# Building the one-hot tables of two edge sums with eight single-value comparisons per turn instead of one wide comparison

## What is computed

```
x = x + gnn0(layernorm(x))        # two layers: h = (x + mean over edges of x[col]) @ W.T + b, norm, silu
x = x + moe(layernorm(x))         # 8 experts, top 2
x = x + gnn1(layernorm(x))        # sum over edges of weight * x[src], two matrices, norm, gelu
x = x + half(layernorm(x))        # a dense part on half of the rows
```

## Time and profile before

| | us |
|---|---|
| median of three runs | 5513.28 |
| lowest and highest run | 5509.91, 5519.62 |
| the profiled execution | 5518.8 |
| its span, first to last instruction | 5517.1 |
| busy in the span: PE, DVE, POOL, ACT | 4292.8, 3152.9, 2684.9, 1286.6 |
| mean granted TensorE clock, as a share of 2.4 GHz | 0.919 |

### The profile page before, as it was taken

How to read it: one execution, slowest core, us unless ns; L and a number is a source line. 1 busy time by engine, 2 the same in 40 slices (tenths; PEclk the granted TensorE clock), 3 DMA queues, 4 the chain that set the end, 5 groups by cost and what they waited for, 6 DMA issues and landing times. The chain is left out here.

```text
span 5517.1 us, 75612 instructions
## 1 busy us (share of the span) xinstructions
PE 4292.8 (78%) x20122; PEld 3546.4 (64%) x20123; DVE 3152.9 (57%) x7387; ACT 1286.6 (23%) x3985; POOL 2684.9 (49%) x2621
## 2 busy tenths in 40 slices
PE   6588777777778888989870699999349888888459
PEld 3386655555557777878760588888237666666347
DVE  8987555555566666766672011111358777787841
ACT  0395000000054434444261122222110000001612
POOL 0003777777717777777705100000457777775121
PEclk9798999999999999999995899999669999999779
DMA  4201333333323333333312312211433333333520
GB/s 171 56 11 38 97 101 103 101 102 100 98 66 93 92 92 92 93 95 94 119 47 74 109 65 68 95 65 67 126 109 104 104 104 104 105 104 89 181 70 18
DMA packets 256142, 499.45 MB, mean 91 GB/s; under 512 B 61573, under 2 KB 149296, under 8 KB 255952
## 3 DMA queue, kind: packets, MB, share of 16 engines
q0 software_dynamic: 125632, 344.11, 21.2%
q1 hardware_dynamic: 125120, 147.87, 8.3%
q10 hardware_dynamic: 5200, 5.24, 0.3%
HBM read 490.49 MB, written 90.68 MB: 105 GB/s over the span
## 5 line engine op out<-in xcount | busy, mean ns | idle before, releaser
L1052 PE MATMUL sum_sums<-sum_got,sum_onehot 128*128 x9408 | 2233.2, 393 | 557.7 <-SPq L114 484.6
L1052 PEld LDWEIGHTS sum_sums<-sum_got,sum_onehot 128*128 128x128 f32 x9408 | 1793.6, 195 | 962.6 <-issue 719.3
L985 POOL DMA_INDIRECT sum_got<-xn,edge_row x1568 | 1539.3, 982 | 1016.8 <-DVE edge_row L1082 491.8
L1255 DVE TENSOR_TENSOR acc<-acc,sum_sums 128x256 f32 (+1 forms) x2352 | 992.0, 422 | 993.1 <-PE sum_sums L1052 739.0
L985 POOL DMA_INDIRECT sum_got<-h,edge_row x784 | 874.8, 1116 | 352.0 <-issue 238.5
L780 ACT ACTIVATE xb<-xb,edge_weight 128x98 f32<-128x98 f32 x1568 | 430.9, 362 | 633.9 <-DVE xb L750 633.3
L1795 POOL DMA_INDIRECT moe_out_c_got<-moe_out,place_i x98 | 95.8, 977 | 881.6 <-PEq L1753 852.1
L1215 DVE TENSOR_TENSOR sum_onehot<-iota,edge_local 128x1024 f32<-128x1024 f32 x396 | 482.8, 1220 | 7.3 <-PEq L2439 7.2
L2026 DVE TENSOR_TENSOR moe_f_y<-moe_f_ps_y,moe_b 128x256 f32<-128x256 f32 x112 | 42.3, 419 | 699.1 <-PE moe_f_ps_y L1961 699.1
L1210 DVE TENSOR_SCALAR sum_onehot<-iota,sum_now 128x128 f32<-128x128 f32 x1584 | 425.0, 360 | 7.5
L1961 PE MATMUL moe_f_ps_y<-xb,moe_f_hT 128*128 128x256 f32 x1792 | 428.7, 382 | 0.0
(11 more groups left out here) (482 smaller groups left out, 3702.2 us busy)
## 6 DMA issues: line engine op xcount, KB each, us to landing
xb<-in_L_ffn_W SPq DMA_DIRECT2D x112, 1024.0 KB
sum_got<-xn,edge_row POOLq DMA_INDIRECT x1568
moe_in<-acc SPq DMA_DIRECT2D x28, 512.0 KB, 6.2
moe_f_xin<-moe_in SPq DMA_DIRECT2D x56, 256.0 KB
moe_out<-moe_f_y SPq DMA_DIRECT2D x56, 256.0 KB
xn<-xb SPq DMA_DIRECT2D x14, 896.0 KB, 8.0
sum_got<-h,edge_row POOLq DMA_INDIRECT x784, 2.8
h<-xb SPq DMA_DIRECT2D x7, 896.0 KB, 4.1
```

The costliest lines, as they stand in the source:

```text
L985: pool.indirect_dma_start(got[:, c % SU, 0:D], None, source, bass.IndirectOffsetOnAxis(ap=p.edge_row[:, c:c + 1], axis=0)).then_inc(s_got[ ...
L1052: mm = nc.tensor.matmul(sums[k % 2][j], onehot[:, ((k % 2) * HALF + j) * PAIR + r, :], pair[:, r, :], start=(r == 0), stop=(r == PAIR - 1))
L1255: v.tensor_tensor(a, a, sums[k % 2][j], ALU.add).then_inc(s_added[j], 1)
```

## The change

The unweighted `build` takes the way of the weighted one. Eight values of `edge_local` are copied to `now` (one field instead of two), a wait on the copy follows, and then come eight `tensor_scalar` comparisons of 128 elements, each against one per-partition value. `now` is allocated in all three passes, with one field where there are no weights. The tables that come out are the same.

```diff
-        now = p.sb("now", [P, 2, 2, HALF * PAIR], F32, ctx) if weighted else None
+        now = p.sb("now", [P, 2, fields, HALF * PAIR], F32, ctx)
...
                 else:
-                    number = p.iota[:].unsqueeze(1).to_broadcast([P, TURN, P])
-                    local = p.edge_local[:, bass.ds(c, TURN)].unsqueeze(2).to_broadcast([P, TURN, P])
-                    ins = v.tensor_tensor(out, number, local, ALU.is_equal)
+                    v.tensor_copy(now[:, half, 0, :], p.edge_local[:, bass.ds(c, TURN)]).then_inc(s_built, 1)
+                    dve.wait_ge(s_built, built)
+                    for j in range(TURN):
+                        ins = v.tensor_scalar(out[:, j, :], p.iota[:], now[:, half, 0, j:j + 1], None, ALU.is_equal)
                 ins.then_inc(s_onehot, 1)
```

## The result

The changed kernel takes 5413.68 us (median of 4 runs, 5410.86 to 5422.98), the kernel before 5515.68 (4 runs, 5509.91 to 5519.62): a ratio of 0.9819, 95% interval 0.9802 to 0.9836, so 102 us less. The forecast was 82 us less, 5431, with a range of 5377 to 5492. The profiled execution of the changed kernel took 5422.98 us, the longest of its four; its span is 5421.2, 95.9 us shorter than before.

The account below looks back on a forecast made before the run. POOL, issuing gathers back to back, was taken to bound sum0 and sum1. 38.4 us (sum0) + 46.7 (sum1) - 2.7 (ends of the passes) = 82.4 us less, bringing the median to 5431, range 5377 to 5492.

Parts of the forecast that it names:

- What bounds the kernel: In sum0 and sum1 POOL issues gathers back to back, 1.251 us each at the median, and sets the pace.
- Rival B: sum1 keeps its length through hosted constructions or DVE and PE; only sum0 gains, 36 us, to 5478; chance 0.15.
- What the wide comparison takes: Gathers wait for comparisons of two SBUF operands, mostly L1215; whole stretch over the median 47.0 us in sum0, 133.3 in sum1.
- What the eight comparisons take: Stretch left by the new comparisons, taken from sum2: 8.6 us for each pass, bounds 0 and 34.
- one of its signs: In sum1 stretched gathers should end 0.82 us after L757 and L750, not after the new comparisons.
- set against itself: Rule that a two-port tensor_scalar fully blocks GpSimd while it runs: 25 us a pass, gain 50 us (5463).
- sum0: Pass with stretch falling from 47.0 to 8.6 us: 38.4 us less on POOL, 1.3 us lost at its start.
- sum1: Pass with 133.3 us of stretch, less 8.6 for new comparisons and 78 for hosted constructions: 46.7 us saved.
- the hosted constructions: L757 and L750 in sum1, 112 each, falling at random places of the gathers' cycle: 78 us, bounds 27.5 and 184.
- Rival C: In sum1 hosted constructions catch gathers from their start, up to 184 us; at the full price 24 us slower, 5537; chance 0.06.
- DVE's side: A build takes 1.81 us, 0.67 more, 131 us more DVE time in each pass; POOL stays the bound.
- Ends of the passes: Builds on the path: 1.3 us ahead of sum0's first matmul, 0.7 behind each pass's last adds; 2.7 us in all.

Follow-up runs that it names:

- hosted_psum: Changed kernel with the hosted column and lane constructions in sum1 reading their numbers from PSUM; 5359.24 us, ratio 0.9708 to the kernel before.
- wide_psum: Changed kernel with one wide comparison of 1024 elements in sum1 again, its column numbers read from PSUM; 5405.28 us, ratio 0.9794 to the kernel before.
- only_sum0: Kernel before with the eight comparisons in sum0 alone, sum1 keeping the wide comparison; 5478.26 us, ratio 0.9925 to the kernel before.
- only_sum1: Kernel before with the eight comparisons in sum1 alone, sum0 keeping the wide comparison; 5454.09 us, ratio 0.9885 to the kernel before.
- two_scalars: Changed kernel with a second per-partition value, a product with one, in each of the eight comparisons; 5413.03 us, ratio 0.9818 to the kernel before.
- short_tt: Changed kernel with the eight comparisons as tensor_tensor of 128 elements, two SBUF operands and no copy; 5474.98 us, ratio 0.9928 to the kernel before.
- all_psum: Changed kernel with sum1's wide comparison back and, like both hosted constructions, reading numbers from PSUM; 5343.47 us, ratio 0.9691 to the kernel before.

## Why the prediction was right, and where its sizes were off

*What bounds the kernel.* Right. POOL issues without a pause before and after, and the table above leaves no room for another bound in `sum1`. Rival B's argument, PE at 1052 of 1163 us, doesn't carry: in `hosted_psum` PE is busy for 953 of 985, and POOL still waits for nothing.

*What the wide comparison takes.* Right in place and in size: the whole stretch is 47.0 and 133.3 us by means, 47.4 and 133.6 added up gather by gather, and 106 of the latter end behind the wide comparison itself. That this comparison holds gathers by reading both its operands from SBUF was only argued then; `wide_psum` shows that with one of them in PSUM it holds none.

*What the eight comparisons take.* Forecast 8.6 us a pass, from `sum2`. Measured 9.3 in `sum0`, of which 7.3 behind the comparisons and the rest in its setup, and 7.1 in `sum1`. The size is right, but the prediction gave no reason for it, and one of its signs failed: stretched gathers should not end 0.82 us after the new comparisons, and 98 and 105 of them do. That such a comparison blocks a gather while it runs, which the prediction set against itself at 25 us a pass, is what the traces show; only the price was too high, by a factor of about three: it took 255 demands a pass as held, and 98 were in `sum0`.

*`sum0`.* Forecast 38.4 us less on POOL and 1.3 back at its start, so 37.1; the pass is 37.1 us shorter.

*`sum1`.* Here is the term that was mis-sized: the hosted constructions. Forecast 78 us if they fall on random places of the gathers' cycle; measured 65.8 (59.0 and 6.8). The split speaks against random places: L757 takes more than its 44 us and L750, with 6.8, far less than its 34. A part of this is the mark itself, which counts a gather held through L750 and L757 wholly to L757 (8 gathers, 10.3 us). The pass gained 60.3 us where 46.7 was forecast; 1.5 us less for the new comparisons and 12.2 for the constructions make this difference of 13.6 us up to rounding. In the seven kernels in which the 224 constructions read both operands from SBUF, they took by that mark 26 (`only_sum0`), 27.5 (before), 55 (`only_sum1`), 59 (`wide_psum`), 65 (`two_scalars`), 66 (after) and 115 us (`short_tt`). In the forecast I let them go from 27.5 to 184 and took the mean of random places; it lies inside what the runs gave, but no closer than tens of microseconds can be asked of it, and that it came within 12 us here is partly luck. Rival C's mechanism, constructions caught nearly from their start, is real: `short_tt` has it, at 115 us of its 184, and loses most of the gain by it. It didn't decide here.

*DVE's side.* 1.77 us a build against 1.81. Costing the extra DVE work at nothing was right, and `two_scalars` shows that even half a microsecond a turn more would have been free.

*Ends of the passes.* The last gather to the next stage's first DVE instruction: 0.6 us more in each pass (from 10.5 to 11.1 behind `sum0`, from 10.1 to 10.7 behind `sum1`), 0.7 forecast.

*The whole.* 82 forecast, 96 by the profiled spans, 102 by the medians. 14 of it is the hosted term and the new comparisons in `sum1`. The last 6 us, between spans and medians, have no cause that a run shows; the profiled execution was the longest of four that differ by 12 us.

## What to carry to other kernels

Where GpSimd issues gathers back to back, look at the longest and the mean of one gather beside its median: the difference times their number is what other engines take from it, and the ends of the stretched ones tell which instruction it was. Two remedies are shown here. An operand moved to PSUM frees the gathers even beside a long instruction: the comparison of 1024 elements held none of the 179 that came to their demand during it in `wide_psum`. Short instructions hold a gather for little: 0.13 us at most behind the eight comparisons of the change. A per-partition value in place of a tensor isn't such a remedy by itself, as the setup of `sum0` shows. The pace of the issuing engine is worth more than time on an engine that waits for it, so more DVE work can make a stage shorter.

## What the runs showed that I had not expected

An operand moved to PSUM costs DVE nothing here: the comparison of 1024 elements took 1217 ns with its numbers in PSUM and 1220 with both operands in SBUF, L757 1079 in `all_psum` against 1085 before. And a gather isn't always let go between two such instructions in a row: in the changed kernel one was held through L750 and L757 together and took 2851 ns, while in the kernel before gathers went on between L1215 and the construction that followed.
